# A fourth probability buffer, a lag of three chunks, and a deferred PSUM copy in the attention loop of a differential-attention block

## The reference, cut to what matters

```python
q1, k1, q2, k2, v = (heads(x @ w.T) for w in (q1_w, k1_w, q2_w, k2_w, v_w))   # 16 heads of 128
attn1 = softmax(q1 @ k1.T / sqrt(128));  attn2 = softmax(q2 @ k2.T / sqrt(128))
out = (attn1 - lam * attn2) @ v
x = layernorm(x + out @ o_w.T)
q, s = per_token_quant_int8(x)
x = layernorm(x + float16((q @ weight.T) * s * w_scale + bias))
```

## Time and profile before

| what | value |
|---|---|
| median of the runs shown | 3184.56 us |
| the profiled execution itself | 3183.85 us |
| its span on the slowest core (core 0) | 3182.3 us |
| spans of the 8 cores | 3176.6 to 3182.3 us |
| PE busy | 2937.6 us, 92% of the span |
| ACT busy | 1302.0 us, 41% |
| DVE busy | 1269.4 us, 40% |

### The profile page before, as it was taken

One profiled execution on the slowest core, in us unless ns is written; L12 is line 12 of the kernel. 1 busy time (PEld: TensorE's weight loads), 2 busy tenths in 40 slices (PEclk: granted clock), 3 DMA queues, 4 the chain that ended last, 5 costly groups with the idle time before them and its releaser, 6 DMA issues.

```text
span 3182.3 us, 45008 instructions; the slowest of 8 cores (3176.6 to 3182.3 us)
## 1 busy us (share of the span) xinstructions
PE 2937.6 (92%) x16640; PEld 1446.6 (45%) x16640; DVE 1269.4 (40%) x1569; ACT 1302.0 (41%) x1363; POOL 44.7 (1%) x85
## 2 busy tenths in 40 slices
PE   0999999999999999999999999999999999896997
PEld 0445454545454545454545454545454544343443
DVE  0123333333333333333333333343434347665676
ACT  0171717171717171717171717070707073444232
POOL 0000000000000000000000000000000000000000
PEclk9999999999999999999999999999999999997998
DMA  9666101111101010101010101010100042436233
GB/s 159 149 182 159 25 17 25 17 24 17 24 15 26 16 26 13 28 14 28 14 27 14 27 13 28 13 28 13 28 1 7 23 131 77 130 109 210 86 109 119
DMA packets 93426, 172.77 MB, mean 54 GB/s; under 512 B 68160, under 2 KB 68160, under 8 KB 86688
## 3 DMA queue, kind: packets, MB, share of 16 engines
q0 software_dynamic: 14016, 86.38, 13.4%
q1 hardware_dynamic: 79200, 83.51, 8.3%
HBM read 174.07 MB, written 50.33 MB: 71 GB/s over the span
## 4 chain that ended last, share of the span: by engine, by line
PE 87%; DVE 4%; ACT 3%; another core or an unknown queue 2%; issue 2%; DMA 1%; DVEq 0%; ACTq 0%; SPq 0%
PE psB L236 14%; PE psA L236 14%; PE psA L253 7%; PE psB L253 7%; PE pO L272 7%; PE pS L274 7%; PE pO L273 7%; PE pS L275 7%; PE psA L224 4%; PE psB L224 4%; PE pffnA L713 4%; PE pffnB L713 3%; ACT pb L302 2%; PE pattnL L499 2%
## 5 line engine op out<-in xcount | busy, mean ns | idle before, releaser
L302 ACT ACTIVATE pb<-psA 128x1024 bf16<-128x1024 f32 x512 | 525.1, 1026 | 1151.4 <-PE psA L253 1151.4
L302 ACT ACTIVATE pb<-psB 128x1024 bf16<-128x1024 f32 x512 | 525.2, 1026 | 121.8 <-PE psB L253 121.8
L236 PE MATMUL psA<-xTb,wq 128*128 128x512 bf16 x2048 | 463.0, 379 | 0.0
L236 PE MATMUL psB<-xTb,wq 128*128 128x512 bf16 x2048 | 462.9, 379 | 0.0
L43 DVE RECIPROCAL r<-sc_ 128x512 f32<-128x512 f32 x128 | 429.1, 3352 | 13.9 <-DVE r L43 0.5
L43 DVE COPY sc_<-pS 128x512 f32<-128x512 f32 x128 | 88.5, 692 | 772.6 <-PE pS L280 766.0
L253 PE MATMUL psA<-q,k 128*128 128x512 bf16 x1024 | 304.4, 379 | 81.4 <-ACT pb L302 80.8
L275 PE MATMUL pS<-pb,ones 128*128 128x512 bf16 x960 | 363.8, 379 | 0.0
L274 PE MATMUL pS<-pb,ones 128*128 128x512 bf16 x960 | 363.8, 379 | 0.0
L273 PE MATMUL pO<-pb,v 128*128 128x512 bf16 x960 | 363.8, 379 | 0.0
L272 PE MATMUL pO<-pb,vv 128*128 128x512 bf16 x960 | 363.7, 379 | 0.0
(11 more groups left out here) (97 smaller groups left out, 2168.7 us busy)
## 6 DMA issues: line engine op xcount, KB each, us to landing
wq<-wqkv POOLq DMA_DIRECT2D x15, 2560.0 KB, 18.6
xin<-x SPq DMA_DIRECT2D x16, 1024.0 KB, 7.5
out<-oo SPq DMA_DIRECT2D x16, 1024.0 KB, 4.8
xTb<-xT POOLq DMA_DIRECT2D x4, 2048.0 KB, 40.8
stg<-wo POOLq DMA_DIRECT2D x16, 512.0 KB, 6.5
wob<-stg SPq DMA_DIRECT2D x16, 512.0 KB, 2.7
stg<-wffn POOLq DMA_DIRECT2D x16, 512.0 KB, 4.2
wfb<-stg SPq DMA_DIRECT2D x16, 512.0 KB, 2.7
```

What stands on the lines that cost most here:

```text
L236: mm = te.matmul(projb[g % 2][:, 0:512], wslice(m + 1, c), xT_sb[:, c * S + qt * 512: c * S + qt * 512 + 512], start=(c == 0), stop=(c == ...
L302: sc.activation(pb_sb[:, (s % 3) * 1024:(s % 3) * 1024 + 1024], sbank[c % 2][:], AF.Exp, scale=INV_SQRT_HD,).then_inc(sEXP, 1)
```

## The change

It does three things.

1. The probability buffer pb has four slots and not three. exp(s) now waits for the product of chunk s-4.
2. PV runs three chunks behind S. A head starts with S(0), S(1), S(2), S(3), PV(0), and ends with four PV in a row.
3. The two ACT copies of pO0 and pO1 of a group move from behind exp(15) to behind exp(2) of the next group, also where that next group is the first one of the next head. Only the copies of the very last group stay at the end.

```diff
-            pb_sb = Eb(nc.sbuf_tensor("pb", [128, 3072], BF16))
+            pb_sb = Eb(nc.sbuf_tensor("pb", [128, 4096], BF16))
...
-                        b = (s % 3) * 1024
+                        b = (s % 4) * 1024
...
                     for k in range(QT * NC_):
                         s_issue(k)
-                        if k >= 2:
-                            pv_issue(k - 2)
+                        if k >= 3:
+                            pv_issue(k - 3)
+                    pv_issue(QT * NC_ - 3)
                     pv_issue(QT * NC_ - 2)
                     pv_issue(QT * NC_ - 1)
 
             @blk.scalar
             def _(sc):
-                for grp in range(H * QT):
-                    for c in range(NC_):
-                        s = grp * NC_ + c
-                        sc.wait_ge(sS, sS_after[(grp, c)])
-                        if s >= 3:
-                            sc.wait_ge(sPVD, s - 2)
-                        sc.activation(
-                            pb_sb[:, (s % 3) * 1024:(s % 3) * 1024 + 1024],
-                            sbank[c % 2][:], AF.Exp,
-                            scale=INV_SQRT_HD,
-                        ).then_inc(sEXP, 1)
+                def ocopy(grp):
                     sc.wait_ge(sPO0, grp + 1)
                     if grp >= 3:
                         sc.wait_ge(sCB, grp - 2)
...
+                for s in range(H * QT * NC_):
+                    grp, c = s // NC_, s % NC_
+                    sc.wait_ge(sS, sS_after[(grp, c)])
+                    if s >= 4:
+                        sc.wait_ge(sPVD, s - 3)
+                    sc.activation(
+                        pb_sb[:, (s % 4) * 1024:(s % 4) * 1024 + 1024],
+                        sbank[c % 2][:], AF.Exp,
+                        scale=INV_SQRT_HD,
+                    ).then_inc(sEXP, 1)
+                    if c == 2 and grp >= 1:
+                        ocopy(grp - 1)
+                ocopy(H * QT - 1)
```

## The result

The changed kernel takes 3201.15 us (median of 11 runs; 10 runs of the kernel before beside them have 3185.12 us). The ratio is 1.0052 with a 95% interval from 1.0041 to 1.0062: 16.0 us slower, where 16.9 were worked out, and under the 2% that this kernel's measurement tells from no change. In some executions of every kernel here four of the cores or all of them had a lower granted clock and took longer; the ratios leave these out, and a time in brackets behind a median is the median without them.

A forecast was written before the change was run, and what follows sets the result against it. PE, with 87% of the chain, was taken to bound the kernel through its matmuls plus gaps. -25.0 + 34.7 + 0.7 + 6.5 = +16.9 us on the median of 3184.56 gave 3201.5 us, range 3185 to 3222.

The forecast's parts named there:

- The group changes: At the 48 group changes inside heads, PE's stall falls from 1.81 to 1.29 us: 48 x 0.52 = 25.0 us saved.
- the 0.25 us in which PE answers DVE: At group changes, PV(0) starts 0.25 us after DVE's copies end, at t+3.02, t being the score pair's start ahead of PV(15).
- Rival A: At the group changes the stall goes altogether, 86.9 us come off: 3133 us; chance 0.05.
- Rival C: At the group changes the stall only moves, the new one equalling the old: 3226 us; chance 0.06.
- The head starts: At the 15 later head starts, PV(0) waits for the deferred copies and S(3) for exp(1): 15 x 2.31 = 34.7 us lost.
- Rival D: At head starts PV(0) is not held by the copies, 22 us less: 3179 us; chance 0.03.
- The clock: At later head starts PE's idling lowers the clock in some, 1.72 us per fall: 15 x 0.25 x 1.72 = 6.5 us lost.
- the share of cores at head 0: 2 of 8 cores showed a lowered clock at head 0; this share was taken for the 15 later head starts.
- Rival B: At every head start the clock falls, and for longer, +58 us: 3243 us; chance 0.06.
- Head 0: At the first head's start PE waits for exp(1) ahead of S(3), with no copies to wait for: 0.7 us lost.
- The sum: Whole kernel: -25.0 + 34.7 + 0.7 + 6.5 = +16.9 us, giving 3201.5 us, +0.5%.

The follow-up runs named there:

- experiment 3: Changed kernel with PV(0)'s wait for DVE's copies moved behind its two pO matmuls, ahead of the first pS matmul; 3201.0 us, ratio 1.0051.
- experiment 7: Kernel of experiment 6 with copies behind exp(0) instead of exp(1), and the wait for DVE's copies ahead of PV(0)'s first pS matmul; 3133.9 us, ratio 0.9839.
- experiment 5: Kernel before (three slots, PV two chunks behind S) with only the ACT copies deferred, behind exp(1) of the next group, also at head starts; 3202.4 us.
- experiment 6: Kernel of experiment 5, but the copies of each head's last group stay behind its exp(15); 3161.7 us, ratio 0.9921.
- experiment 1: Changed kernel with the copies of each head's last group put back behind exp(15), the other 48 still deferred; 3173.9 us, ratio 0.9966.
- experiment 4: Changed kernel with the edit of experiment 3 plus six thrown-away matmuls between S(3) and PV(0) of heads 1 to 15; 3190.3 us, ratio 1.0003.
- experiment 8: Kernel of experiment 7 with a wait for each of four PSUM tensors, PV(15) and PV(0) in the order pS0, pO0, pS1, pO1; 3129.8 us, ratio 0.9813.

## Why the prediction was right

**The group changes** (48 x 0.52 = 25.0 us saved). Right in size and in cause: the stall is 1.29 us, two group ends came 0.53 us closer, and DVE ends the wait 0.13 us after ACT would (experiment 3). One term was lucky: I took the 0.25 us in which PE answers DVE from the k cast at a head start, and experiment 7 shows 0.15 us for another instruction. In both places one more wait stands behind the one for DVE, which the prediction didn't look at (see the last section). Rivals A and C are out: PV(0) nowhere follows its score pair at once, and it waits 1.1 us at most group changes (50.4 us at the 44 that end by DVE); only two of them have 1.47 us, which is t+3.4. That the gain is all of the copies' place on ACT and none of the lag or the fourth slot was said only of the slot; experiments 5 and 6 show it of both.

**The head starts** (15 x 2.31 = 34.7 us lost). Right: PV(0) 5.08 us behind S(0) for 5.09, S(3) at 3.20 for 3.19, and a head without a fall is 0.71 us longer for 0.75. Experiment 1 splits it: with the copies put back 1.45 us of it goes, 0.8 stays as the price of the lag. Rival D is out; it needed the head-end copies where experiment 1 puts them.

**The clock** (15 x 0.25 x 1.72 = 6.5 us). The price was right (1.67 us), and so was the number, 3.9 falls a core for 3.75. But the step that gave the number, the share of cores at head 0, was weaker than its result looks: the same head start had 8 falls a core in experiment 3, and in experiment 5 one that idles less (0.85, 0.20 and 1.82 us within 4.2 us) had about 9. Head 0 itself fell on two of eight cores before, on four after and on none to three in the experiments. The prediction also read the old head starts as idling 1.5 us; the earlier trace rows give 0.85 + 0.20 = 1.05 us, which changes no term. The share was right by luck within a factor of two, which the range (0 to 26 us) covered. Rival B, a costlier fall at every head start, did not occur: every fall in these heads lasted 3.4 us. The Trainium skill (TensorE: Matmul & The Clock Gate, section "HAM oscillation — how this bites in real kernels") pictures a fall for every burst, in a kernel that waits about 3 to 5 us between bursts. The runs show its price, half of the throttled time (1.67 us of 3.4), but with single gaps of at most 1.82 us there are falls at 3 to 10 of the 15 head starts, and at none once the idling was filled.

**Head 0** (0.7 us). Nearly right: from exp(0) to exp(0) it became 0.98 us shorter where the clock didn't fall; its three group changes gave 3 x 0.52 = 1.56 us, so its start costs 0.58 us. The prediction had no term for more falls there: two more cores fell, at 159.56 - 158.20 = 1.36 us each, 0.3 us a core.

**The sum.** From the head lengths it is 15 x 0.71 + 3.9 x 1.67 - 0.98 (head 0) = 16.2 us, against 16.0 us between the medians. The mean over the cores of the stretch from exp(0) of head 0 to exp(0) of head 15 grew by 15.2 us (2388.4 to 2403.6); the last head's own part comes on top.

## What to carry to other kernels

When a buffer's evacuation is deferred past the next work on the same engine, ask what it is deferred past at every boundary: inside a head it left the path, at a head start it landed on it, and the sign of the whole change was decided there. Ahead of deepening a pipeline, look which wait is the last in each stall; here it was the reading of four PSUM tensors with one wait in front of all, and splitting that wait, with the copies behind exp(0), took the stall from 1.29 to 0.53 us, more than the 0.52 us of the deferral alone. And in a chain so tight the next wait stands close behind the freed one (0.13 us in experiment 3), or the reordering makes a new one (0.41 us in experiment 8), so each step has to be worked out to the instruction behind the one that was freed.

## What the runs showed of the hardware that I had not expected

- How often the clock falls depends on more than the idle time. With PE idling in pieces of 0.85, 0.20, 0.85 and about 1.47 us at a head start, the changed kernel, with a head of 159.8 us, had 3 or 4 falls in 15 heads and experiment 3, with the same head start and a head of 159.4 us, had 7 or 8, on all cores. What makes the number was not tested. A saving of 6.2 us was hidden by this in full, and came out when the idle time was filled with six thrown-away matmuls (experiment 4). A comparison of such kernels has to count the falls ahead of reading the difference.
- How soon PE goes on after another engine's end depends on where that wait stands. PE went on 0.15 us after the end of a DVE copy where the wait for it was the last ahead of the matmul (experiment 7: 996.25 to 996.40), and 0.25 us after where one more wait stood behind it (the changed kernel's group change, and the k cast in the earlier trace rows). The number of waits doesn't make it: at the changed kernel's head start the same PV(0) with the same three waits, but with ACT's, the last of them, ending last, starts 0.14 us after ACT's end (1110.04 to 1110.18). And at head 0 of the kernel before, where S(1) waits for the k cast alone (the wait for exp starts with S(2)), the cast ends at 149.30 and S(1) starts at 149.45, 0.15 us later and not 0.25. No run changes the order of the waits alone.
